# An exponential moved to an earlier table switch, gather rows for empty slots, and expert numbers loaded in two pieces

## The chip, the cores and the metric

The program runs on one core of one Trainium2 chip. The metric is the device time of one execution in microseconds (us). The decoder has six stages; the change touches only the third, the first expert layer.

## What is computed

The reference is a decoder of two layers on x of shape (8, 256, 128), which are 2,048 tokens of width 128. The stage at hand is the routed and shared feed-forward of the first layer:

```
D_MODEL, HIDDEN, E_ROUTED, E_SHARED, TOP_K = 128, 256, 14, 2, 2
def _ffn(xn, rw, W1, W2):
    h = xn * rsqrt(mean(xn * xn) + RMS_EPS) * rw
    return silu(h @ W1) @ W2
```

Each token goes through both shared experts and through the two of 14 routed experts with the largest router logits. The routed results are weighted by gates: a softmax over the 14 logits, of which the two chosen are kept and divided by their sum. A layer norm of x plus this sum ends the stage.

## The kernel before

**The routing.** Tokens are sorted by expert into slots, 128 to a tile. NT is 45, the most tiles that 4,096 choices can need when each of 14 experts ends with a tile that is not full. VectorE (DVE) finds the rank of each choice (`RANK`, `TOTAL`, lines 1579 to 1629), and TensorE (PE) sums one-hot matrices into `SLOT_TOK`, the token number of each slot (line 2311). A slot that nobody has stays at 0, and so it names token 0. `tok` (line 1631) is the copy of these numbers, and `tei` (line 1635) holds for each tile the offset of its expert's weights.

**The gates.** DVE writes the scaled logits `Lg` (lines 1537 and 1541, semaphore `lg_sub`). ScalarE (ACT) takes the exponential (line 1063, semaphore `lg_exp`). The rest of the gates (`gates_step` 2 and on) is done by DVE between tiles 6 and 20 of the tile loop.

**The shared experts.** PE's `shared_up(n)` (line 2285), ACT's `shared_silu(n)` (line 1053) and PE's `shared_out(n)` (line 2291) run for n from 0 to 7 ahead of the tile loop, beside DVE's routing, and for n from 8 to 15 behind it. After each of the first eight Silus ACT normalizes two tiles of X (line 1069). The exponential stands behind Silu number 7, the last ahead of the tile loop. ACT's functions come in tables: an ACT_TABLE_LOAD stands in the trace where another table is loaded.

**The tile loop.** POOL issues one indirect DMA for each tile j (line 815), which gathers 128 rows of `xrows` into `XG[j % 4]` by `tok[:, j]`. For i from 0 to 47, PE issues in this order:

```
slot_up(i - 1)        # hidden = xTs @ W1E[expert], line 2346; waits for ACT's Silu of the tile before
experts_from(i)       # if i % 4 == 0: load the next 4 offsets from tei, line 2337
gather_T(i)           # transpose of XG, line 2333; waits for the gather
hidden_T(i - 2)       # lines 2352, 2353
slot_down(i - 3)      # y = hidden @ W2E[expert], line 2360
```

DVE copies the transposes out of PSUM (`xTs` line 1685, `hTs` line 1690), ACT takes the Silu into `hS` (line 1075) and copies `Y` (line 1081), and SP stores each Y. Ahead of its first tile ACT also copies the sums of the shared experts (`OT`, line 1057). When all Ys are stored POOL gathers them back (line 821).

The order on each engine is written out by hand. The functions that the diff touches:

Of the kernel before, what the change touches and what calls it, by code (L numbers as in the profile page):

```python
# [19 lines left out]
ACT = mybir.ActivationFunctionType  # L20
AX = mybir.AxisListType
F32 = mybir.dt.float32
# [3 lines left out]
F16 = mybir.dt.float16  # L26
# [4 lines left out]
T = N // 128  # L31
# [8 lines left out]
E1, I1, K1 = 64, 64, 8  # L40
NT = (2 * N + E0R * 127) // 128
RING = 4
SPLITS = 12
FAR = 8192.0
ROUND = 12582912.0
# [4 lines left out]
def decoder_program(nc, a, out):  # L50
# [28 lines left out]
        "route_consts": ("norm_done", B * PAIRS + 2),  # L79
        "route_init": ("split_done", B // 2 * SPLITS + 2),  # L80
        "yt_ready": ("fold_hi", 4),
        "xs_out": ("raw_in0", B * SPLITS // 4 * 16),
        "we_in": ("raw_in1", B * SPLITS // 4 * 16),
        "decay_out": ("split_out0", B * SPLITS // 4 * 16),
        "coef_out": ("split_out1", B * SPLITS // 4 * 16),
        "te_done": ("acc_free", B + 2),
# [4 lines left out]
        "sum_done": ("rms", 2 * NC_ + 2),  # L91
        "hot_j": ("w_rounded", B // 2 * SPLITS),
        "shared_added": ("bo_added", 4),
        "ya_in0": ("xg_in0", (NT + 3) // RING * 16),
        "ya_in1": ("xg_in1", (NT + 2) // RING * 16),
        "ya_in2": ("xg_in2", (NT + 1) // RING * 16),
        "ya_in3": ("xg_in3", NT // RING * 16),
        "diag_done": ("q_done", 4),
# [11 lines left out]
    def sem(name):  # L110
        name = COUNTS_ON[name][0] if name in COUNTS_ON else name
        if name not in sems:
            sems[name] = ctx.enter_context(nc.semaphore(name))
        return sems[name]

    def on(name, n):
        return COUNTS_ON[name][1] + n

    def sb(name, shape, dt=F32, scope=ctx):
        return scope.enter_context(nc.sbuf_tensor(name, shape, dt))  # L120

    with ctx:
        PS = ctx.enter_context(nc.psum_tensor("PS", [128, 8 * CH], F32))

        def bank(n, w=CH, k=1):
            return PS[:, n * CH:n * CH + (k - 1) * CH + w]
# [117 lines left out]
        sx = ExitStack()  # L244
        eqJ = sb("eqJ", [128, 2, NT, T], F16, sx)
        idJ = sb("idJ", [128, 2, NT, T], F16, sx)
# [1 line left out]
        iotaR = sb("iotaR", [128, 128, T], F16, sx)  # L248
        jslot16 = sb("jslot16", [128, 2, T], F16, sx)
        rslot16 = sb("rslot16", [128, 2, T], F16, sx)  # L250
        tokid16 = sb("tokid16", [128, T], F16, sx)
        cmpJ = sb("cmpJ", [128, NT, E0R], F32, sx)
        Lg = sb("Lg", [128, T, E0R], F32, sx)
        eqE = sb("eqE", [128, T, E0R], F32, sx)
# [11 lines left out]
        over = sb("over", [128, E0R, T], F32, sx)  # L266
# [8 lines left out]
        tok = sb("tok", [128, NT], U32, sx)  # L275
        iota128 = sb("iota128", [128, 128], F32, sx)
        iotaJ = sb("iotaJ", [128, NT], F32, sx)
        iotaK = sb("iotaK", [128, T], F32, sx)
        tokid = sb("tokid", [128, T], F32, sx)
        notfirst = sb("notfirst", [128, E0R, T], F32, sx)  # L280
        below = sb("below", [128, 128], F32, sx)
        XG = [sb(f"XG{r}", [128, 128], F32, sx) for r in range(RING)]
        xTs = [sb(f"xTs{r}", [128, 128], F32, sx) for r in range(2)]
        hS = [sb(f"hS{r}", [128, HID], F32, sx) for r in range(2)]
        hTs = [sb(f"hTs{r}", [128, HID], F32, sx) for r in range(2)]
        Y = [sb(f"Y{r}", [128, 128], F32, sx) for r in range(RING)]
        kTe = sb("kTe", [128, B * SC], F32, sx)
# [85 lines left out]
        SLOT_TOK = bank(7)[:, 256:256 + NT]  # L373
# [47 lines left out]
            return bank(4 + t // 4)[:, t % 4 * 128:t % 4 * 128 + 128]  # L421


        GATES_EXP = 7
        FIRST, LAST = 0, B // 2 - 1
        RANKS_AT, HOT_AT = 0, {5: (0, 1), 6: (2, 3)}
        STEPS = 2 * PAIRS
# [5 lines left out]
        def turn(n, c):  # L433
            return NC_ * n + c + (B - NC_ if n > 2 else 0)
# [232 lines left out]
        def _(pool):  # L667
# [8 lines left out]
                               base=0, pattern=[[-1, 128]], channel_multiplier=1).then_inc(sem("consts"), 1)  # L676
            pool.affine_select(out=cmask[:, 128:256], in_=cmask[:, 128:256], compare_op=ALU.is_ge, fill=BIG,
                               base=0, pattern=[[-1, 128]], channel_multiplier=1).then_inc(sem("consts"), 1)
            pool.affine_select(out=blockones[:, :], in_=blockones[:, :], compare_op=ALU.is_ge, fill=0.0,
                               base=0, pattern=[[-DX, HX], [0, DX]], channel_multiplier=1).then_inc(sem("zeroed"), 1)  # L680
            pool.wait_ge(sem("zeroed"), 4)
            pool.affine_select(out=blockones[:, :], in_=blockones[:, :], compare_op=ALU.is_ge, fill=0.0,
                               base=DX - 1, pattern=[[DX, HX], [0, DX]], channel_multiplier=-1).then_inc(sem("consts"), 1)
# [95 lines left out]
            for s in range(2):  # L779
# [2 lines left out]
            pool.iota(iota128[:, :], [[1, 128]], base=0, channel_multiplier=0, allow_small_or_imprecise_dtypes=True).then_inc(sem("route_consts"), 1)  # L782
            pool.iota(iotaJ[:, :], [[1, NT]], base=0, channel_multiplier=0, allow_small_or_imprecise_dtypes=True).then_inc(sem("route_consts"), 1)
            pool.iota(iotaK[:, :], [[128, T]], base=0, channel_multiplier=0, allow_small_or_imprecise_dtypes=True).then_inc(sem("route_consts"), 1)
            pool.iota(tokid[:, :], [[128, T]], base=0, channel_multiplier=1, allow_small_or_imprecise_dtypes=True).then_inc(sem("route_consts"), 1)
            pool.memset(notfirst[:, :, :], 1.0).then_inc(sem("route_init"), 1)
            pool.memset(below[:, :], -1.0).then_inc(sem("route_init"), 1)
            pool.memset(G20[:, :, :], NEG).then_inc(sem("route_consts"), 1)
# [4 lines left out]
                               base=0, pattern=[[-1, 128]], channel_multiplier=1).then_inc(sem("route_consts"), 1)  # L793
            pool.wait_ge(sem("route_consts"), on("route_consts", 8))
            pool.tensor_copy(iotaR[:, :, :], iota128[:, :].rearrange("p (r o) -> p r o", o=1).to_broadcast([128, 128, T])).then_inc(sem("route_consts"), 1)
            pool.tensor_copy(tokid16[:, :], tokid[:, :]).then_inc(sem("route_consts"), 1)

            for c in range(NC_):
                cc = slice(4 * c, 4 * c + 4)
# [10 lines left out]
            pool.wait_ge(sem("tok_done"), on("tok_done", 1))  # L810
            pool.wait_ge(sem("xs_out"), on("xs_out", 16 * NC_))
            for j in range(NT):
                if j >= RING:
                    pool.wait_ge(sem("xt_ready"), on("xt_ready", j - RING + 1))
                pool.indirect_dma_start(out=XG[j % RING][:, :], out_offset=None, in_=xrows,  # L815
                                        in_offset=bass.IndirectOffsetOnAxis(ap=tok[:, j:j + 1], axis=0)).then_inc(sem(f"xg_in{j % RING}"), 16)
# [95 lines left out]
        def _(act):  # L912
# [146 lines left out]
            for n in range(8):  # L1059
                shared_silu(n)  # L1060
                if n == GATES_EXP:
                    act.wait_ge(sem("lg_sub"), 1)
                    act.activation(Lg[:, :, :], Lg[:, :, :], ACT.Exp).then_inc(sem("lg_exp"), 1)
                if n % 2 == 0:
                    act.wait_ge(sem("ln_factor"), 2 * turn(1, n // 2) + 2)
                if n == 4:
                    act.wait_ge(sem("xs_late"), 8)
                for t in (2 * n, 2 * n + 1):
                    act.activation(X[:, t, :], X[:, t, :], ACT.Identity, scale=rs[:, t:t + 1], bias=nb[:, t:t + 1]).then_inc(sem("ln_x"), 1)

            def slot_silu(j):
                act.wait_ge(sem("hs_ready"), on("hs_ready", j + 1))
# [234 lines left out]
        def _(dve):  # L1307
# [195 lines left out]
            def after_last():  # L1503
                dve.wait_ge(sem("g_step"), steps[0])

            def done(instruction):
                instruction.then_inc(sem("g_step"), 1)
                steps[0] += 1
# [67 lines left out]
            flat2 = lambda x: x.rearrange("p e t -> p (e t)")  # L1576
# [35 lines left out]
            across = lambda x, w: x.rearrange("p (o t) -> p o t", o=1).to_broadcast([128, w, x.shape[-1]])  # L1612
# [6 lines left out]
            for s in range(2):  # L1619
                if s:  # L1620
                    same_tile(1)
                dve.wait_ge(sem("hot_j"), on("hot_j", s + 1))
                done(dve.tensor_tensor(idJ[:, s, :, :], eqJ[:, s, :, :], across(tokid16[:, :], NT), ALU.mult))
                after_last()
                for h in range(2):
                    tt = slice(8 * h, 8 * h + 8)
                    dve.tensor_tensor(eqH[:, s, :, tt], iotaR[:, :, tt], across(rslot16[:, s, tt], 128), ALU.is_equal).then_inc(sem("hot_done"), 1)
            done(dve.tensor_tensor(cmpJ[:, :, :], iotaJ[:, :].rearrange("p (j o) -> p j o", o=1).to_broadcast([128, NT, E0R]),
                                   ctile[:, :].rearrange("p (o e) -> p o e", o=1).to_broadcast([128, NT, E0R]), ALU.is_ge))
            dve.wait_ge(sem("tok_ready"), 1)  # L1630
            dve.tensor_copy(tok[:, :], SLOT_TOK).then_inc(sem("tok_done"), 1)  # L1631
            after_last()
            done(dve.tensor_reduce(te[:, :], cmpJ[:, :, :], AX.X, ALU.add))
            after_last()
            dve.tensor_scalar(tei[:, :], te[:, :], float(E0R - 1), float(HID), ALU.min, ALU.mult).then_inc(sem("te_done"), 1)
# [405 lines left out]
            with dve.Fori(2, E1 // 4) as i:  # L2041
                for k in range(8):
# [6 lines left out]
                    s, c = k // 4, k % 4  # L2049
# [11 lines left out]
        def _(pe):  # L2061
# [271 lines left out]
                pe.transpose(slot_xT, XG[j % RING][:, :], ident[:, :]).then_inc(sem("xt_ready"), 1)  # L2333

            def experts_from(j):
                n = min(NT - j, 4)
                _, e = nc.values_load_multi_w_load_instructions(
                    tei[0:1, j:j + n], engines=[mybir.EngineType.PE], min_val=0, max_val=(E0R - 1) * HID,
                    skip_runtime_bounds_check_because="a count of at least 0, bounded by ALU.min where tei is written")
                return {j + m: e[m] for m in range(n)}  # L2340
# [24 lines left out]
            for i in range(NT + 3):  # L2365
                if 1 <= i < NT + 1:
                    slot_up(i - 1, experts[i - 1])
                if i < NT:
                    if i % 4 == 0:
                        experts.update(experts_from(i))  # L2370
                    gather_T(i)
                if 2 <= i < NT + 2:
                    hidden_T(i - 2)
                if i >= 3:
                    slot_down(i - 3, experts.pop(i - 3))
                if 2 <= i < 4:
                    shared_T(i - 2, i - 2)
# [405 lines left out]
```

## Time and profile before

| | |
|---|---|
| runs | 954.63, 954.72, 957.13 us; median 954.72 |
| profiled execution | 955.09 us, span 953.0 us |
| busy | PE 883.2 us, DVE 779.8, ACT 557.4, POOL 419.4 |
| mean granted PE clock | 0.977 |
| tile loop, first to last transpose of XG | 332.3 to 404.1 us |

The span is the time from the first instruction to the last, and the 2.09 us beside it are start and end of the execution. Busy time of PE is not PE at its peak, since matmuls overlap. The chain of work says which engine each moment of the end time hung on.

### The profile page before, as it was taken

How to read it: one execution, taken by the hardware profiler on the slowest of the kernel's cores; microseconds unless marked ns; L12 is line 12 of the kernel's file. 1: busy time of each engine (PE TensorE's matmuls, PEld its weight loads, DVE VectorE, ACT ScalarE, POOL GpSimd, SP SyncE). 2: the span in 40 equal slices, each digit the busy share in tenths (PEclk: the TensorE clock that was granted, in tenths of full speed). 3: DMA queues.
4: the chain of work that ended last, by engine and by line, in shares of the span. 5: the costliest groups of instructions: out<-in, count | busy, mean ns of one | idle time of the engine just before them, and what ended most of it. 6: DMA issues, size and time to landing. Idle time of an engine off the chain costs nothing.

```text
span 953.0 us, 17273 instructions
## 1 busy us (share of the span) xinstructions
PE 883.2 (93%) x5277; PEld 720.8 (76%) x5277; DVE 779.8 (82%) x2047; ACT 557.4 (58%) x1323; POOL 419.4 (44%) x491
## 2 busy tenths in 40 slices
PE   6999999999998888889877999989999999999995
PEld 5888888888886467747765797876668888888883
DVE  5887888889988657728898999968599999999996
ACT  5666666667767543447874324356755565556555
POOL 6776767667766165456416577432710000000002
PEclk9999999999999899999998899999999999999998
DMA  8333323233225033511012211010056666666641
GB/s 310 114 112 98 108 94 122 96 102 114 92 96 182 6 73 84 76 47 34 23 46 90 73 61 45 1 50 17 6 155 182 182 174 177 174 179 173 181 137 44
DMA packets 47280, 98.46 MB, mean 103 GB/s; under 512 B 7137, under 2 KB 23585, under 8 KB 46194
## 3 DMA queue, kind: packets, MB, share of 16 engines
q1 hardware_dynamic: 44754, 92.64, 31.6%
q0 software_dynamic: 2464, 5.05, 2.9%
q8 instruction: 32, 0.52, 0.2%
q14 instruction: 30, 0.25, 0.1%
HBM read 75.25 MB, written 22.41 MB: 102 GB/s over the span
## 4 chain that ended last, share of the span: by engine, by line
PE 72%; DVE 15%; issue 6%; ACT 3%; DMA 2%; POOL 1%; another core or an unknown queue 1%; DVEq 0%; SPq 0%; POOLq 0%; ACTq 0%
PE PS L2063 16%; PE PS L2064 15%; PE PS L2065 15%; PE PS L2134 5%; PE PS L2122 5%; DVE rb L1860 3%; PE PS L2146 3%; PE PS L2360 3%; DVE keep L1841 2%; PE PS L2346 2%; PE PS L2285 2%; PE PS L2291 1%; DVE PS L1829 1%; DVE dfb L1846 1%; DMA W<-w3s 1%
## 5 line engine op out<-in xcount | busy, mean ns | idle before, releaser
L460 POOL TENSOR_TENSOR rs<-ms,neghalf 128x4 f32<-128x4 f32 (+1 forms) x28 | 26.0, 928 | 273.2 <-DVE nm L454 271.5
L708 POOL TENSOR_TENSOR P<-P,rl 128x256 f32<-128x256 f32 (+1 forms) x128 | 104.2, 835 | 71.0 <-DVE rl L1365 71.0
L1292 ACT ACTIVATE FG<-PS 128x512 f32<-128x512 f32 x112 | 66.9, 597 | 92.9 <-PE PS L2065 92.9
L941 ACT ACTIVATE P<-P,mn 128x128 f32<-128x128 f32 (+1 forms) x256 | 112.6, 444 | 0.4 <-DVE mn L1358 0.4
L2063 PE MATMUL PS<-XTh,W 128*128 128x512 f32 x256 | 100.5, 393 | 1.5 <-DMA W<-w3s 0.6
L2064 PE MATMUL PS<-XTl,W 128*128 128x512 f32 x256 | 99.7, 390 | 0.0
L2065 PE MATMUL PS<-XTh,W 128*128 128x512 f32 x256 | 99.7, 390 | 0.0
L2046 DVE TENSOR_TENSOR FU<-FG,PS 128x512 f32<-128x512 f32 x112 | 77.0, 688 | 17.4 <-ACT FG L1292 4.6
L1358 DVE CUSTOM_DVE_ANT_0 P<-PS,cmask 128x128 f32<-128x128 f32 (+1 forms) x256 | 75.9, 352 | 18.6 <-issue 18.4
L2029 DVE TENSOR_TENSOR FHL<-FH,FHH 128x512 fp32r<-128x512 f32 x128 | 89.9, 702 | 0.9 <-ACT FHH L1278 0.9
L948 ACT ACTIVATE Uh<-PS 128x512 fp32r<-128x512 f32 x64 | 38.3, 598 | 81.9 <-PE PS L2065 81.8
L1278 ACT ACTIVATE FHH<-FH 128x512 fp32r<-128x512 f32 x128 | 80.9, 632 | 8.2 <-DVE FH L2038 7.8
L1370 DVE COPY PT<-PS 128x768 f32<-128x768 f32 x64 | 60.3, 942 | 7.5 <-PE PS L2122 7.4
L815 POOL DMA_INDIRECT XG<-xrows,tok x45 | 42.8, 951 | 45.7 <-DVE tok L1631 19.0
L2063 PEld LDWEIGHTS PS<-XTh,W 128*128 128x128 f32 x256 | 48.0, 188 | 16.2 <-issue 5.9
L2065 PEld LDWEIGHTS PS<-XTh,W 128*128 128x128 f32 x256 | 48.1, 188 | 10.1
L2122 PE MATMUL PS<-ident,P 128*128 128x128 f32 x384 | 54.4, 278 | 1.0 <-POOL P L708 0.9
L850 POOL TENSOR_TENSOR gb<-gb,dfb 128x1020 f32<-128x1020 f32 x16 | 37.9, 2386 | 38.9 <-ACT dfb L1207 38.5
L2064 PEld LDWEIGHTS PS<-XTl,W 128*128 128x128 f32 x256 | 48.1, 188 | 9.1
L2063 PE MATMUL PS<-FHH,W 128*128 128x512 f32 x128 | 50.9, 398 | 1.1 <-DVE FHL L2029 0.8
L1388 DVE TENSOR_TENSOR Ul<-PS,Uh 128x512 fp32r<-128x512 f32 x64 | 44.2, 691 | 8.6 <-ACT Uh L948 0.2
L2065 PE MATMUL PS<-FHH,W 128*128 128x512 f32 x128 | 49.9, 390 | 0.0
(472 smaller groups left out, 2559.1 us busy)
## 6 DMA issues: line engine op xcount, KB each, us to landing
GI<-coef SPq DMA_DIRECT2D x56, 256.0 KB, 4.1
GW<-coef SPq DMA_DIRECT2D x56, 256.0 KB, 4.1
w3s<-WS SPq DMA_DIRECT2D x32, 384.0 KB, 2.6
W<-w3s SPq DMA_DIRECT2D x32, 384.0 KB, 3.3
Wb<-decay SPq DMA_DIRECT2D x7, 1024.0 KB, 4.7
WR<-in_w SPq DMA_DIRECT2D x32, 192.0 KB, 2.5
WR<-in_w SPq DMA_DIRECT2D x16, 256.0 KB, 2.9
w12f<-WS SPq DMA_DIRECT2D x16, 256.0 KB, 2.0
```

Of the source, the lines that this page charges most:

```text
L708: last = pool.tensor_tensor(v, v, f, ALU.mult)
L941: last = act.activation(P[:, slot, c:c + w], P[:, slot, c:c + w], ACT.Exp, scale=-1.0, bias=mn[:, par, q:q + 1], accum_out=ls[:, par, q:q ...
L1278: act.activation(FHH[:, (k - 1) % 4, :], FH[:, (k - 1) % 4, :], ACT.Copy).then_inc(sem("fhh_done"), 1)
L1292: act.activation(FG[:, k % 2, :], bank(4 + k % 2), ACT.Silu).then_inc(sem("fg_done"), 1)
L1358: dve.tensor_tensor_reduce(out=P[:, slot, c:c + w], in0=scores(par, q), in1=cmask[:, 256 - w:256], scale=1.0, scalar=3e38, op0=ALU.add, op ...
L1370: dve.tensor_copy(PT[:, k % 2, :, :], PTP).then_inc(sem("pt_done"), 1)
L2029: dve.tensor_tensor(FHL[:, (k - 1) % 4, :], FH[:, (k - 1) % 4, :], FHH[:, (k - 1) % 4, :].bitcast(F32), ALU.subtract).then_inc(sem("fhl_do ...
L2046: dve.tensor_tensor(FU[:, k % 2, :], FG[:, k % 2, :], bank(6 + k % 2), ALU.mult).then_inc(sem("ft_done"), 1)
L2063: pe.matmul(dst, l[0], r[0], start=start, stop=False, skip_group_check=skip)
L2064: pe.matmul(dst, l[0], r[1], start=False, stop=False, skip_group_check=skip)
L2065: return pe.matmul(dst, l[1], r[0], start=False, stop=stop, skip_group_check=skip)
L2122: last = pe.transpose(bank(4 + h)[:, j * 128:j * 128 + 128], P[:, slot, c:c + 128], ident[:, :])
```

## The change

Three edits, all in the first expert layer.

- The exponential of the gates moves from behind Silu number 7 to behind Silu number 0, after the two tiles of X that are normalized there. The tables are loaded by two explicit instructions, for Exp ahead of these normalizations and for Silu behind the exponential.
- The token numbers are written plus one, so that an empty slot shows as 0. The first 4 tiles get max(number - 1, 0), as before. In tiles 4 to 44 a slot with 0 gets its own partition's number p, so that its gather reads row p of `xrows` and not row 0. This makes three DVE instructions of one, and POOL waits for the second part ahead of tile 4. Empty slots' results are read by nobody.
- The offsets are loaded 23 and then 22 at a time (i = 0 and 23), where they were loaded 4 at a time (12 loads).

```diff
+READY_TILES = 4
+NE = (NT + 1) // 2
...
-        GATES_EXP = 7
+        GATES_EXP = 0
...
-            pool.iota(tokid[:, :], [[128, T]], base=0, channel_multiplier=1, ...)
+            pool.iota(nextid[:, :], [[128, T]], base=1, channel_multiplier=1, ...)
...
             for j in range(NT):
+                if j == READY_TILES:
+                    pool.wait_ge(sem("tok_done"), on("tok_done", 2))
                 if j >= RING:
                     pool.wait_ge(sem("xt_ready"), on("xt_ready", j - RING + 1))
...
             for n in range(8):
                 shared_silu(n)
                 if n == GATES_EXP:
-                    act.wait_ge(sem("lg_sub"), 1)
-                    act.activation(Lg[:, :, :], Lg[:, :, :], ACT.Exp).then_inc(sem("lg_exp"), 1)
+                    act.preload_act_table(ACT.Exp)
...
                 for t in (2 * n, 2 * n + 1):
                     act.activation(X[:, t, :], X[:, t, :], ACT.Identity, ...)
+                if n == GATES_EXP:
+                    act.wait_ge(sem("lg_sub"), 1)
+                    act.activation(Lg[:, :, :], Lg[:, :, :], ACT.Exp).then_inc(sem("lg_exp"), 1)
+                    act.preload_act_table(ACT.Silu)
...
-                done(dve.tensor_tensor(idJ[:, s, :, :], eqJ[:, s, :, :], across(tokid16[:, :], NT), ALU.mult))
+                done(dve.tensor_tensor(idJ[:, s, :, :], eqJ[:, s, :, :], across(next16[:, :], NT), ALU.mult))
...
-            dve.tensor_copy(tok[:, :], SLOT_TOK).then_inc(sem("tok_done"), 1)
+            dve.tensor_scalar(tok[:, 0:READY_TILES], SLOT_TOK[:, 0:READY_TILES], -1.0, 0.0, ALU.add, ALU.max).then_inc(sem("tok_done"), 1)
+            own_row = flat2(over[:, :, :])[:, READY_TILES:NT]
+            done(dve.scalar_tensor_tensor(own_row, SLOT_TOK[:, READY_TILES:], 0.0, nextid[:, 0:1].to_broadcast([128, NT - READY_TILES]), ALU.is_equal, ALU.mult))
             after_last()
+            dve.scalar_tensor_tensor(tok[:, READY_TILES:], SLOT_TOK[:, READY_TILES:], -1.0, own_row, ALU.add, ALU.add).then_inc(sem("tok_done"), 1)
             done(dve.tensor_reduce(te[:, :], cmpJ[:, :, :], AX.X, ALU.add))
...
-                n = min(NT - j, 4)
+                n = min(NT - j, NE)
...
-                    if i % 4 == 0:
+                    if i % NE == 0:
                         experts.update(experts_from(i))
```

## Rows read from the trace of the kernel before

**Rows 1.** The page: the span, and the chain that ended last by engine.

```profile
span 953.0 us, 17273 instructions
...
PE 72%; DVE 15%; issue 6%; ACT 3%; DMA 2%; POOL 1%; another core or an unknown queue 1%; DVEq 0%; SPq 0%; POOLq 0%; ACTq 0%
```

**Rows 2.** The chain of work around the start of the tile loop: start, length, what.

```profile
330.36 1.28 ACT L1063
...
331.65 0.39 ACT Lg L1063
332.04 0.77 ACT Xp L1069 x2
332.81 0.96 ACT OT L1057 x2
...
333.79 1.28 ACT L1075
...
335.08 0.39 ACT hS L1075
```

**Rows 3.** PE in order of time: start, length, what, and idle time with its releaser.

```profile
333.05 0.69 PE L2346 MATMUL PS<-W1E,xTs 128*128 x2 [0.46 <-DVE xTs L1685]
...
335.70 0.69 PE L2346 MATMUL PS<-W1E,xTs 128*128 x2 [1.85 <-ACT hS L1075]
```

**Rows 4.** ACT in order of time around the first two shared Silus.

```profile
310.98 0.60 ACT L1053 ACTIVATE Hf<-PS 128x512 f32<-128x512 f32 x1 [2.40 <-PE PS L2285]
...
316.77 0.60 ACT L1053 ACTIVATE Hf<-PS 128x512 f32<-128x512 f32 x1 [4.43 <-PE PS L2285]
```

**Rows 5.** DVE in order of time: scaled logits, then token numbers and expert offsets.

```profile
313.42 0.39 DVE L1541 TENSOR_TENSOR Lg<-Lg,rs 128x224 f32<-128x224 f32 x1
...
328.85 0.21 DVE L1631 CAST tok<-PS 128x45 uint32<-128x45 f32 x1 [2.97 <-PE PS L2311]
328.97 0.80 DVE L1633 TENSOR_REDUCE te<-cmpJ 128x45 f32<-128x630 f32 x1
329.81 0.19 DVE L1635 TENSOR_SCALAR tei<-te 128x45 int32<-128x45 f32 x1
```

**Rows 6.** The gathered tile XG: PE's transposes of it (ns min/median/max, first and last start).

```profile
L2333 PE MATMUL PS<-ident,XG x45: 272/273/329, 332.3 to 404.1; 128*128 128x128 f32 x45
```

**Rows 7.** PE in order of time in the tile loop, tiles 11 to 13, 34, 35 and 43.

```profile
351.11 0.27 PE L2333 MATMUL PS<-ident,XG 128*128 128x128 f32 x1
...
352.46 0.29 PE L2333 MATMUL PS<-ident,XG 128*128 128x128 f32 x1
...
353.97 0.68 PE L2360 MATMUL PS<-W2E,hTs 128*128 x4 [0.99 <-ACT Y L1081]
...
354.93 0.27 PE L2333 MATMUL PS<-ident,XG 128*128 128x128 f32 x1
...
387.44 0.27 PE L2333 MATMUL PS<-ident,XG 128*128 128x128 f32 x1
...
389.87 0.27 PE L2333 MATMUL PS<-ident,XG 128*128 128x128 f32 x1
...
402.78 0.33 PE L2333 MATMUL PS<-ident,XG 128*128 128x128 f32 x1 [0.57 <-DMA XG<-xrows,tok]
```

**Rows 8.** Loads of expert offsets (ns min/median/max, first and last start): all, the one-value load.

```profile
L2337 PEldq TENSOR_LOAD <-tei x12: 313/334/517, 330.4 to 403.6; - x12
...
L2337 PEldq TENSOR_LOAD <-tei x1: 313/313/313, 403.6 to 403.6; - x1
```

**Rows 9.** Stretches: length, busy (instructions) of PE, PEld, DVE, ACT, POOL, clock, DMA share, GB/s.

```profile
383.00:393.00 10.00, 8.82 (x59) 7.33 (x58) 6.64 (x24) 3.99 (x13) 5.85 (x7) 1.00 0.34 78
...
398.00:403.00 5.00, 3.99 (x26) 2.88 (x25) 3.45 (x9) 1.98 (x6) 0.88 (x1) 1.00 0.88 58
```

**Rows 10.** The chain of work at the loop's tail and behind it.

```profile
396.65 6.08 DMA XG<-xrows,tok
...
408.89 2.67 PE PS L2285 x6
```

More of the change, by code:

```diff
@@ L250, in decoder_program @@
         rslot16 = sb("rslot16", [128, 2, T], F16, sx)
-        tokid16 = sb("tokid16", [128, T], F16, sx)
+        next16 = sb("next16", [128, T], F16, sx)
         cmpJ = sb("cmpJ", [128, NT, E0R], F32, sx)
@@ L278, in decoder_program @@
         iotaK = sb("iotaK", [128, T], F32, sx)
-        tokid = sb("tokid", [128, T], F32, sx)
+        nextid = sb("nextid", [128, T], F32, sx)
         notfirst = sb("notfirst", [128, E0R, T], F32, sx)
@@ L784, in _ @@
             pool.iota(iotaK[:, :], [[128, T]], base=0, channel_multiplier=0, allow_small_or_imprecise_dtypes=True).then_inc(sem("route_consts"), 1)
-            pool.iota(tokid[:, :], [[128, T]], base=0, channel_multiplier=1, allow_small_or_imprecise_dtypes=True).then_inc(sem("route_consts"), 1)
+            pool.iota(nextid[:, :], [[128, T]], base=1, channel_multiplier=1, allow_small_or_imprecise_dtypes=True).then_inc(sem("route_consts"), 1)
             pool.memset(notfirst[:, :, :], 1.0).then_inc(sem("route_init"), 1)
@@ L795, in _ @@
             pool.tensor_copy(iotaR[:, :, :], iota128[:, :].rearrange("p (r o) -> p r o", o=1).to_broadcast([128, 128, T])).then_inc(sem("route_consts"), 1)
-            pool.tensor_copy(tokid16[:, :], tokid[:, :]).then_inc(sem("route_consts"), 1)
+            pool.tensor_copy(next16[:, :], nextid[:, :]).then_inc(sem("route_consts"), 1)
             for c in range(NC_):
```

## Prediction

> **What bounds the kernel now.** I read the page first. The chain that ended last is PE for 72% and DVE for 15% [rows 1], but that is an average over six stages, and the change touches only one, between about 311 and 409 us. So I read the chain of work and PE in order of time there. Three stretches of that stage matter.
>
> At the start of the tile loop the chain lies on ACT. Behind the last shared Silu it loads a table (1.28 us), takes the exponential (0.39), normalizes two tiles (0.77), copies two sums (0.96), loads the Silu table again (1.28), and only then takes the first tile's Silu at 335.08 [rows 2]. PE's second slot_up stands idle for 1.85 us until that Silu is there [rows 3].
>
> In the middle of the loop PE sets the pace. The transposes of XG, one a tile, follow each other at 1.35 us when nothing disturbs (351.11 to 352.46), which is PE's own work for a tile [rows 7]. All 45 take 404.1 - 332.3 = 71.8 us [rows 6], while 44 steps of 1.35 are 59.4 us. The other 12.4 us are disturbances. The largest kind looks like tile 12 to 13: 2.47 us, or 1.1 over the pace, in which slot_down idles 0.99 us for a copy of Y that itself waited for an earlier result of PE [rows 7]. I went through the 44 steps. Six are of that kind, from tiles 4, 12, 16, 20, 28 and 34, with 1.0 to 1.7 us over the pace each. Some others are 0.3 us over.
>
> At the loop's tail the chain hangs for 6.08 us on one gather, issued at 396.65 [rows 10]. In that stretch the DMA engines are 88% busy and move 58 GB/s. Ten us earlier, with the same size of gathers, they were 34% busy and moved 78 GB/s [rows 9]. The last tiles are the empty ones, and all their 128 slots name row 0, so repeated reads of one row are what I take as the cause.
>
> Behind the loop PE goes straight into the second half of the shared experts [rows 10]. So what the loop saves is passed on to the rest of the program, which has no part in the change.
>
> **Part 1, the exponential.** Removed from the stretch before the loop: one table load (1.28) and the exponential (0.39) behind Silu 7, and the Silu load (1.28) ahead of the first tile, 2.95 us of ACT work [rows 2]. The gain is smaller than that, since other waits come next. The copies of the two sums need the last shared_out, which ends at about 332.3, just ahead of the first transpose of XG [rows 6]. They then take 0.96 and end at 333.3. The first tile's Silu needs slot_up, which starts at 333.05 and takes 0.69, so it can start at about 333.8 [rows 3]. It starts at 335.08 now. The gain is 335.08 - 333.8 = 1.3 us. What is late next is PE, then the gathers: POOL issues the first eight 1.25 us apart, slightly faster than PE's 1.35, so I count nothing for them.
>
> What is added lies beside the first two Silus. Silu 0 ends at 311.58 and Silu 1 starts at 316.77, with ACT idle for 4.43 us because it waits for PE [rows 4]. The added sequence is: table load 311.6 to 312.9, two normalizations to 313.7 (0.77), the wait for the logits that DVE ends at 313.81 [rows 5], exponential to 314.3, table load to 315.5. That leaves 1.2 us of cover. Should it be gone, each us past it delays Silu 1, and shared_out 1 behind it. Nobody needs the exponential before tile 6.
>
> **Part 2, rows for empty slots.** The first part of `tok` is a short tensor_scalar in place of the 0.21 us copy [rows 5]. The nearest small DVE instruction is the tei one, 0.19 us, so the first gather starts as before. Two more DVE instructions of about 0.2 us and a wait of 0.05 lie ahead of te and tei: +0.45 us, and tei ends at 330.45 and not at 330.0. PE's first load of offsets starts at 330.4 now and is the longest of the twelve, 0.52 [rows 8]; and the next thing on PE is the first transpose at 332.3, which waits for its gather [rows 6]. The load would end at about 331.4, so 0.9 us of cover is left and the cost is nothing. POOL's new wait ahead of tile 4 is over by about 329.5, while the fifth gather is issued at 334.6. Nothing queues behind it.
>
> The gain is at the tail. The steps 39 to 43 are 1.80, 1.42, 1.93, 2.05 and 1.32 us, together 1.8 over the pace; for two of them PE waits in so many words for the gather, 0.44 us at tile 42 and 0.57 at tile 43 [rows 7]. Lower bound 0, if the slowness has another cause. Upper bound 1.8. I take 1.2, since the first 0.45 came while its gather had long landed.
>
> **Part 3, two loads for twelve.** The instruction itself is cheap: 334 ns in the median, nearly all for four values [rows 8], and at tile 12 the transposes around it are on the pace, 351.11 and 352.46 [rows 7]. So by the direct cost, ten loads are worth about nothing. But the disturbance of 1.1 us follows at once. Of the six long ones five (tiles 4, 12, 16, 20, 28) come in the tile that has a load, though only one tile in four has one; and five loads (tiles 8, 24, 32, 36, 40) have none behind them. The sixth, tile 34 to 35 (387.44 to 389.87), looks the same and has no load near [rows 7]. I read this as a hold-up of PE's results that arises by itself every two to four tiles, short (0.3 us) when nothing else is there and long when a load falls into it. Lower bound of the gain: 0, if the holds don't care about the loads. Upper bound: the five long ones whole, 1.74 + 1.11 + 1.00 + 0.96 + 1.11 = 5.9 us. If each turned into a short one, 5.9 - 1.5 = 4.4. The case of tile 34 says that long ones come without loads too, so I take 2.5.
>
> The new loads carry 23 and 22 values. The median of 334 ns is that of loads of four values, and the one of a single value took 313 [rows 8]: 7 ns for each further value, which makes about 0.5 us for 23. The first is under the cover of part 2, the second costs at most 0.5 at tile 23, inside the 2.5.
>
> The Trainium skill (Runtime: NRT & Kernel Launch, section Instruction fetch mechanics) gives about 200 ns per register for a load of registers, even in bulk. The trace does not agree: four values would be 0.8 us, and the row has 0.33. What the skill's figure would make of the sum is given with the rivals.
>
> **The sum.** 1.3 + 1.2 + 2.5 = 5.0 us. The profiled execution has 955.09 us (span 953.0 and 2.09 around it), which becomes 950.1. It is 0.37 above the median of the runs, so against the median of 954.72 the forecast is 949.7. Less than about 0.3% (2.9 us) can't be told from no change in this kernel.
>
> **The rivals.**
> - *The holds don't care about the loads.* Then part 3 gives 0 to 0.9 and the sum is 1.0 to 3.4 us: about 952.3, between 951.3 and 953.7. For it: tile 34, and the five loads without a hold. It also covers that a loop without loads runs into its holds more often: 16 to 20 was four tiles at 1.6 us each, and the whole loop at that rate would give back some 1.5 us. Against it: five of six. Chance 0.37.
> - *The holds need the loads altogether.* All the excess between tiles 4 and 39 goes, some 7 us, and the sum is 8 to 10: about 945.5. Against it: tile 34 and the short ones. Chance 0.09.
> - *Repeated reads are not the cause of the slow tail.* Parts 1 and 3 are left, 3.8 us: 950.9. For it: only that no row shows a gather of 128 distinct rows with this neighbourhood. Against it: the same gathers ran at 34% share just before [rows 9]. Chance 0.05. The edit would then not do what it says.
> - *The long loads stop PE* (the other side). If the values are fetched one after another at the price of the one-value load, 0.313 us [rows 8], the first takes 7.2 us and ends at 337.7, 5.4 after 332.3, and the second adds 6.9 at tile 23. With the 5.0 of gain that is 7.3 slower: 962.0. It decides from about 0.2 us for each value. Against it: four values cost as much as one. Chance 0.05.
>
> By the 200 ns of the Trainium skill (Runtime: NRT & Kernel Launch, Instruction fetch mechanics) the loads would take 4.6 and 4.4 us, which ends at about 957; the trace's 334 ns for four values speaks against it.
>
> **How the numbers follow.** The forecast (sum 3.5 to 8, 946.7 to 951.2) has 0.44. The likeliest single time is 949.7. The range must leave out no more than 2 in 10: from 945.5 (most of the second rival) to 953.4 (most of the first). Faster by over 0.3% needs a gain of 2.9: the forecast 0.44, the second rival 0.09, of the first about 0.05, of the third 0.03, together 0.61. Slower by over 0.3% is the last rival and whatever the phase of PE's clock in the later stages may cost: 0.05. Within 0.3%: 0.34.
>
> **What the profile after would show.** Part 1: two table loads between Silu 0 and Silu 1 near 312 and 315, none between 329 and 400, and hS of tile 0 at about 333.8. Part 2: the last steps at the pace, no wait for XG there, a DMA share of about 0.35 up to the end of the loop, tei at about 330.5. Part 3: two TENSOR_LOADs of about 0.5 us; fewer or shorter holds, and the first to the last transpose in 67 to 68 us and not 71.8. The prediction is wrong if the holds stand as many and as long in a loop without loads, or if a TENSOR_LOAD of 23 values is long.

## The result, and the profile after

The changed kernel takes 961.45 us in the median of four runs (959.77 to 962.88), the kernel before 954.71 beside it (954.63 to 957.13, four runs). The ratio is 1.0068, 95% interval 1.0047 to 1.0090: it is slower, by 6.5 us at that ratio. The forecast was 949.7 with a range of 945.5 to 953.4, so the sign is wrong, and of the rivals the one to which I gave 0.05 has come closest (962.0).

The profiled execution took 959.77 us. First the page, to be held against [rows 1]:

```profile
span 957.8 us, 17266 instructions
...
PE 71%; DVE 13%; issue 6%; ACT 4%; POOL 3%; DMA 2%; another core or an unknown queue 1%; SPq 0%; DVEq 0%; POOLq 0%; ACTq 0%
```

It says nothing of the cause: the shares are nearly those of before. The two other edits did what was said. ACT in order of time around the first two Silus, for [rows 4]:

```profile
312.21 0.60 ACT L1057 ACTIVATE Hf<-PS 128x512 f32<-128x512 f32 x1 [2.52 <-PE PS L2295]
312.83 1.28 ACT L1066 ACT_TABLE_LOAD   x1
314.12 0.88 ACT L1072 ACTIVATE Xp<-Xp,nb,rs 128x128 f32<-128x128 f32 x2
314.94 0.39 ACT L1075 ACTIVATE Lg<-Lg 128x224 f32<-128x224 f32 x1
315.35 1.28 ACT L1076 ACT_TABLE_LOAD   x1
317.87 0.60 ACT L1057 ACTIVATE Hf<-PS 128x512 f32<-128x512 f32 x1 [1.24 <-PE PS L2295]
```

All of the exponential's work lies in the gap between Silu 0 and Silu 1, and 1.24 us of cover is left (1.2 was forecast). PE's first slot_ups, for [rows 3]:

```profile
334.82 0.69 PE L2356 MATMUL PS<-W1E,xTs 128*128 x2 [0.46 <-DVE xTs L1695]
...
336.17 0.69 PE L2356 MATMUL PS<-W1E,xTs 128*128 x2 [0.55 <-DVE xTs L1695]
```

They are 1.35 us apart and were 2.65: 1.3 us gained, as in the sum. Then two stretches near the loop's end, for [rows 9] (length, busy of PE, PEld, DVE, ACT, POOL, clock, DMA share, GB/s):

```profile
389.00:399.00 10.00, 9.38 (x63) 7.90 (x61) 7.05 (x25) 4.48 (x14) 5.91 (x7) 1.00 0.31 83
404.00:409.00 5.00, 4.93 (x33) 4.20 (x33) 4.09 (x13) 2.31 (x8) 1.58 (x2) 1.00 0.33 92
```

The last tiles' gathers now cost the DMA engines no more than the others do: share 0.33 and 92 GB/s, where it was 0.88 and 58. The chain has no wait for a gather there any more, where it had one of 6.08 us [rows 10].

The third edit is where the time went. The loads of offsets and the transposes (ns min/median/max, first and last start), for [rows 8] and [rows 6]:

```profile
L2347 PEldq TENSOR_LOAD <-tei x1: 2282/2282/2282, 331.6 to 331.6; - x1
...
L2347 PEldq TENSOR_LOAD <-tei x1: 5258/5258/5258, 371.8 to 371.8; - x1
...
L2343 PE MATMUL PS<-ident,XG x45: 272/273/447, 334.1 to 410.1; 128*128 128x128 f32 x45
```

The load of 23 values takes 2.28 us and that of 22 takes 5.26, where I had 0.5 for each. The 45 transposes take 76.0 us; 67 to 68 were forecast, and 71.8 it was before. PE in order of time at the second load, for [rows 7], and the stretch behind it:

```profile
371.01 0.27 PE L2343 MATMUL PS<-ident,XG 128*128 128x128 f32 x1
...
371.83 0.69 PE L2356 MATMUL PS<-W1E,xTs 128*128 x2
377.27 0.45 PE L2343 MATMUL PS<-ident,XG 128*128 128x128 f32 x1 [4.75 <-issue]
...
379.65 0.42 PE L2343 MATMUL PS<-ident,XG 128*128 128x128 f32 x1
...
381.13 0.27 PE L2343 MATMUL PS<-ident,XG 128*128 128x128 f32 x1
```

```profile
376.80:380.20 3.40, 2.93 (x12) 2.67 (x13) 1.25 (x5) 0.59 (x2) 0.94 (x1) 0.50 0.10 26
```

PE idles for 4.75 us with "issue" as the reason, which is to say that its own queue was busy, with the load. Then it works for 3.4 us at a granted clock of 0.50, the lower of its two levels (1.2 GHz), after having stood idle. The step from tile 22 to 23 takes 377.27 - 371.01 = 6.26 us and the next 2.38, which is 4.91 and 1.03 over the pace of 1.35. The first load delays the first transpose by 0.8 (it stands 3.7 us behind the first gather's issue, and 2.9 before). Together 6.7 us lost, 1.3 gained at the first tiles, and 1.6 at the tail, whose steps 39 to 43 take 6.94 us and took 8.52: 3.8 us.

There is a second stretch at half clock, with no load near. At tiles 4 and 5 two PE instructions wait 0.84 and 1.00 us, and then PE works at 0.50 up to about 346.1 (transposes, and the stretch):

```profile
339.70 0.27 PE L2343 MATMUL PS<-ident,XG 128*128 128x128 f32 x1
...
343.82 0.42 PE L2343 MATMUL PS<-ident,XG 128*128 128x128 f32 x1
...
346.13 0.27 PE L2343 MATMUL PS<-ident,XG 128*128 128x128 f32 x1
```

```profile
342.80:346.10 3.30, 3.30 (x13) 2.79 (x13) 1.57 (x4) 0.94 (x3) 1.16 (x2) 0.50 0.26 65
```

The steps from tiles 4 and 5 take 4.12 and 2.31 us, and 3.09 and 1.35 before: 2.0 us more. That these are a consequence of the change is not shown. In all, the time from the first gather's issue to the last transpose has grown by 5.0 us (79.7 from 74.7); ahead of it the profiled execution is 1.0 us longer, and behind it 1.2 us shorter.

The holds that I had put down to the loads are still there. The changed kernel has long steps from tiles 4, 12, 16 and 20, as the kernel before has, with loads at tiles 0 and 23 only.

### The profile page after: what moved, and what is told of

Same layout as the page of the kernel before. It is cut to its first block, busy times and chain, and to the rows that moved or that the text cites. A ratio compares the mean times of both kernels' runs of the same rounds, so it can differ in the third digit from the quotient of the medians.

```text
span 957.8 us, 17266 instructions
## 1 busy us (share of the span) xinstructions
PE 887.8 (93%) x5277; PEld 727.4 (76%) x5277; DVE 780.8 (82%) x2049; ACT 556.7 (58%) x1323; POOL 419.4 (44%) x491
## 4 chain that ended last, share of the span: by engine, by line
PE 71%; DVE 13%; issue 6%; ACT 4%; POOL 3%; DMA 2%; another core or an unknown queue 1%; SPq 0%; DVEq 0%; POOLq 0%; ACTq 0%
PE PS L2073 15%; PE PS L2075 14%; PE PS L2074 14%; PE PS L2144 5%; PE PS L2132 5%; PE PS L2370 3%; PE PS L2156 3%; DVE rb L1870 2%; PE PS L2356 2%; DVE keep L1851 2%; PE PS L2295 1%; PE PS L2301 1%; DMA WR<-in_w 1%; DMA W<-w3s 1%; DVE dfb L1856 1%
```

## Experiments

Ratios are against the kernel before on the same chip, with 95% intervals. Kernels without a ratio ran once, so their times have no interval. The runs fell on several chips, and that turned out to matter: the kernel before takes 954.4 to 954.7 us on some of them (three at least) and 943.8 (one run) and 944.9 on two others. Each chip had one batch of runs, so chip and batch are not told apart. A "hold" is a step of the loop that is about 1 us over the pace because PE's results come late.

**The parts by themselves.** Each is that part of the change's diff and nothing else. For the kernel with the first two parts:

```diff
 READY_TILES = 4
-NE = (NT + 1) // 2
+NE = 4
```

*The exponential alone.* 

> The kernel before with part 1 alone. If part 1 is worth what was forecast, the first tile's Silu starts 1.3 us earlier against the first transpose of XG and the time falls by 1.3 us, to about 953.4. Rival, that the tighter start costs something (a hold-up in the first tiles, or a half-speed stretch of PE's clock there): no gain or a loss, 954.7 or more.

Measured: 954.65, ratio 1.0001 (0.9987 to 1.0015). The first slot_ups are 1.35 us apart, but the third and the fifth step have become longer, 1.90 and 3.55 where they were 1.35 and 3.09. Of the 1.3 us about 0.2 is left by then. From the first gather's issue to the last transpose the loop takes 73.65 us and took 74.73, and what stands behind it takes 550.5 in this execution and took 548.9.

*The rows for empty slots alone.* 

> The kernel before with part 2 alone. If repeated reads of row 0 slow the tail, steps 39 to 43 of the loop fall from 8.5 us together to about 6.8 and the time by 1.2 to 1.8, to about 953.2. Rival, that the two more DVE instructions delay the first tile: the first transpose of XG is 0.4 us later and nothing is gained.

Measured: 953.5, ratio 0.9985 (0.9973 to 0.9997), 1.4 us faster; the tail's steps are 1.35 to 1.40.

*The two long loads alone.* 

> The kernel before with part 3 alone. If the long loads are what made the changed kernel slower, it takes all of the loss and what parts 1 and 2 gave back: 6.7 + 2.8 = 9.5 us, about 964, with loads of 2 to 5 us again. Rival, that parts 1 or 2 have a share in the loss: below 960.

Measured: 958.18, ratio 1.0038 (1.0023 to 1.0052). Loads of 2.28 and 5.26 us, the step of tile 22 is 6.26. So this edit alone makes the kernel slower, by 3.6 us. That is far from the 9.5 that I expected, and about half of what the changed kernel loses: beside the other two parts the loads cost more than alone.

*The first two parts, loads of four.* 

> The changed kernel with four values a load again, so parts 1 and 2 without 3. If the long loads are the loss: 1.3 + 1.5 = 2.8 us below the kernel before, about 951.9. Rival, that another part is the loss: 956 or more.

Measured: 954.46, ratio 1.0004 (0.9991 to 1.0018). Without the long loads the loss is gone, but the 2.5 us forecast for the other two parts aren't there: the interval allows 0.9. In its trace the first gather to the last transpose takes 73.73 us, 1.0 less than before.

**Do the holds hang on the loads, or on PE's instructions?** Loads of 8 and of 12 values, no loads at all, and more waits per tile, each in the kernel before:

```diff
-                n = min(NT - j, 4)
+                n = min(NT - j, 8)      # or 12, 16
...
-                    if i % 4 == 0:
+                    if i % 8 == 0:      # or 12, 16
```

```diff
-                    if i % 4 == 0:
-                        experts.update(experts_from(i))
+                    experts[i] = 0      # and constant offsets in slot_up and slot_down
```

```diff
+                for _ in range(10):
+                    pe.wait_ge(sem("te_done"), on("te_done", 1))
```

> The kernel before with 8 values a load (6 loads). Loads of 4 took 0.33 us, of 22 and 23 values 5.26 and 2.28. If a load's price goes by its number of values, loads of 8 take 0.6 to 1.8 us each. If it stays flat up to some number, they take 0.35 us. The time stays within 3 us of before either way.

> The kernel before with 12 values a load (4 loads). By the number of values: 1.1 to 2.8 us each in the loop, at 0.1 to 0.24 us for each value. If the second long load was slow because of what runs beside it in the loop, the loads at tiles 12, 24 and 36 take twice as long as the one at tile 0 or more. If it was slow for another reason, all of 12 values take the same.

> The kernel before with every tile using the first expert's weights at a fixed place: no loads of offsets and no address arithmetic on PE, and the routed results are other than the reference's. If the holds of PE's results come from the loads, they go and the loop runs at 1.35 us a tile from tile 5 on, some 8 us less. If they don't, the mean stays near 1.58 us a tile. If they come from the rate at which PE takes instructions (about 25 records a tile), 2 to 3 fewer a tile give about 1.4 to 1.45.

> The kernel before with ten more waits a tile on PE, for a semaphore that has long been reached (five more sequencer instructions a tile, 0.05 us each, beside the wait for xTs). If the mean step is set by the number of PE's instructions (25 a tile in 1.58 us), 30 a tile make it 1.9 us and the loop 14 us longer. If not, it stays between 1.6 and 1.7.

Measured, with before at 954.45: 956.46, 959.34, 952.49 and 961.02. A load of 8 takes 0.60 us in most cases, one of 12 takes 0.86 and 0.96 behind the first tile. The third kernel has no load and shorter steps, 1.24 us when nothing disturbs, but its loop is no faster than 1.56 a tile, because it has as many holds and longer ones (2.5 to 2.6 us steps). Its transposes take as long as those of before:

```profile
L2333 PE MATMUL PS<-ident,XG x45: 272/273/421, 330.9 to 401.6; 128*128 128x128 f32 x45
```

So the holds do not need loads, which ends my reading of "five of six". The fourth kernel has an undisturbed step of 1.48 us and a mean of 1.66 from tile 5 to 21: its ten more waits do not stretch the mean to the 1.9 that a price for each of PE's instructions would give. Of the 6.6 us that it is slower, about 3.1 lie in the loop (77.9 us from the first gather's issue to the last transpose) and 3.7 behind it, where nothing was changed (552.5 us, and 548.9 before); why, no run shows.

**Loads of 16, gathers off POOL, six small loads at once.** These three fell on a chip where before takes 943.8 us.

> The kernel before with 16 values a load (16, 16 and 13, at tiles 0, 16 and 32). Loads of 4, 8 and 12 values in the loop took 0.33, 0.60 and 0.9 us, about 0.07 us for each value past the fourth. If that line goes on, 16 values take 1.15 us in the loop and 1.3 at tile 0. If a steeper part begins between 12 and 22 values, as 2.28 and 5.26 us for 23 and 22 say, they take 1.5 us or more; and if it is the second load that is slow, the one at tile 16 takes over twice the one at tile 0.

> The kernel before with the rows of XG brought by SP's queue, 128 rows in order and not by token, where POOL issued indirect gathers; the routed results are other than the reference's. All variants so far ran tiles 5 to 39 at 1.55 to 1.66 us each, with holds of PE's results between steps of 1.24 to 1.48. If the gathers issued by POOL cause the holds, they go and the mean is about 1.36. If PE's own work or the stores of Y do, the mean stays at 1.57.

> The changed kernel's grouping (23 values at tile 0, 22 at tile 23) on the kernel before, but each group fetched by six loads of up to four values in a row. If the price belongs to the single long instruction, six times 0.33 us, 2.0 us in all at either place. If it belongs to the number of values fetched at one place, the group at tile 23 takes 5 us again.

```diff
-            for j in range(NT):     # POOL: indirect_dma_start by tok[:, j]
+            def rows_in(j):         # SP: rows in their order
+                sp.dma_start(XG[j % RING][:, :], xrows[j % 16 * 128:j % 16 * 128 + 128, :]) ...
```

```diff
+                for k in range(j, min(NT, j + 23), 4):
+                    n = min(NT, j + 23, k + 4) - k      # a load of n <= 4, six at j = 0, six at j = 23
```

Measured: 945.63, 940.25 and 951.4. None of the three has a hold. From tile 4 on their loops run at the pace of 1.35, but for the steps at the loads and, where empty slots read row 0, the last ones. Gathers that POOL issues do not suffice for a hold, then. Whether they have a part in the holds on the other chips is not shown, since the kernel without them ran only here, where no kernel has holds. The loads of 16 take 1.30 us (the first) and 1.12, and the last, of 13, takes 1.12. The six small loads at tile 0 take 0.53, 0.35, 0.34, 0.33, 0.33 and then 0.77 for three values; those at tile 23 take 1.01, 1.15, 1.00, 1.00, 1.00 and 0.53. They do the same work as the six before and cost three times as much. So it isn't the length of one load that makes 22 values dear.

**What makes a load dear?** Four kernels with other groups of values. A correction to their expectations, which speak of the changed kernel: all four are the kernel before with its loads regrouped and nothing else (neither the exponential's move nor the rows). What they say of single loads isn't touched by it, but their times are to be held against the kernel before and against the long loads alone (958.18), and not against the changed kernel.

```diff
-                n = min(NT - j, 4)
+                n = STARTS[j]           # GROUPS = [23, 4, 4, 4, 4, 4, 2], or [4, 4, 4, 4, 4, 3, 22],
...                                      # or [24, 21], or [6, 4, 4, 4, 4, 4, 4, 4, 4, 4, 3]
-                    if i % 4 == 0:
+                    if i in STARTS:
```

> The changed kernel with the same first load of 23 expert numbers ahead of tile 0, but from tile 23 on in loads of 4 as in the kernel before (six small loads). Theory A, the number of values in one load sets its price: the 23 take 2.28 us as before and the small ones about 0.33 us each; the half-clock stretch behind tile 22 goes and the time falls by 5 to 7 us against the changed kernel. Theory B, once 23 values have been loaded every later load is dear (0.25 us per value): the small ones take about 1.0 us each, as the six small loads at tile 23 did, and the time stays within 3 us of the changed kernel's.

> The mirror image: loads of 4 for tiles 0 to 22 as in the kernel before, then one load of 22 ahead of tile 23. Theory A, 22 values in one load are dear by their number: 5.3 us at tile 23 as in the changed kernel. Theory B, only an earlier long load makes the second dear: about 22 x 0.07 = 1.5 us, and no half-clock stretch behind it. Theory C, the place (tile 23, in the midst of the loop's work) makes it dear: 5.3 us too, so A and C are not told apart by this run alone but by the small loads at the same place in the first kernel of this call.

The times are 946.42 and 951.71, with before at 944.92. The loads in the first kernel (23; the five of 4; the 2) and in the second (five of 4; the 3; the 22):

```profile
L2340 PEldq TENSOR_LOAD <-tei x1: 2289/2289/2289, 329.5 to 329.5; - x1
...
L2340 PEldq TENSOR_LOAD <-tei x5: 1002/1003/1122, 363.5 to 387.7; - x5
...
L2340 PEldq TENSOR_LOAD <-tei x1: 534/534/534, 393.7 to 393.7; - x1
```

```profile
L2340 PEldq TENSOR_LOAD <-tei x5: 330/336/529, 329.9 to 354.5; - x5
...
L2340 PEldq TENSOR_LOAD <-tei x1: 772/772/772, 360.0 to 360.0; - x1
...
L2340 PEldq TENSOR_LOAD <-tei x1: 5268/5268/5268, 364.4 to 364.4; - x1
```

Neither theory stands. Small loads are dear from tile 23 on (against A), and the 22 values are dear with no long load before them (against B). Nor is it the moment in the loop (C), since 16 values at tile 16 take 1.12 us. What fits nearly all of them is the place of the first value. From a multiple of four, each whole four costs about 0.28 us and each value left over 0.26; from another place, every value costs about 0.25. By it 23 from 0 is 5 x 0.28 + 3 x 0.26 = 2.18 (2.28 measured; a first load takes 0.1 to 0.2 more than later ones), 22 from 23 is 5.5 (5.26), 4 from 23 is 1.0 (1.00), 3 from 20 is 0.78 (0.77), 13 from 32 is 1.10 (1.12). Beside the 22, the worst fit is the last load of the kernel with loads of 8, 5 values from 40: 0.54 by the rule, and 0.72 measured. The other two kernels put it to the test.

> The changed kernel with its expert numbers in two loads of 24 and 21 in place of 23 and 22, so that the second begins at value 24, a multiple of four. The durations so far (4 values 0.33, 8 0.60, 12 0.86, 16 1.12, 13 beginning at 32 1.12; but 22 beginning at 23 5.26, 4 beginning at 23 1.0, 3 beginning at 20 0.77) fit a rule: from a first value whose place is a multiple of four, each whole four costs about 0.28 us and each left over 0.26; from another place every value costs about 0.25. By it the loads take 24: 6 x 0.28 = 1.7 us, and 0.2 more as a first load, and 21: 5 x 0.28 + 0.26 = 1.7 us, the half-clock stretch behind the second goes, and the kernel is about 4 us faster than the changed one. Rival, the number of values or the registers that they go to make the second dear: 5 us at tile 23 again, a half-clock stretch behind it, and the changed kernel's time.

> The changed kernel with a first load of 6 values and then loads of 4 that begin at 6, 10, 14 and so on, never at a multiple of four; no load is long. By the rule of the place (fours only from a multiple of four) the first takes 0.28 + 2 x 0.26 + 0.2 = 1.0 us and each of the others 1.0 us in place of 0.33; if pairs count too, each of the others takes about 0.55. Rival, an earlier long load makes later ones dear: 0.33 us each here.

```profile
L2340 PEldq TENSOR_LOAD <-tei x2: 1705/1756/1808, 331.3 to 372.5; - x2
```

```profile
L2340 PEldq TENSOR_LOAD <-tei x11: 763/1002/1123, 329.3 to 401.4; - x11
```

Both as by the rule: 24 values in 1.81 us and 21 in 1.71 with no stretch at half clock behind them; and 1.0 us for each four values from 6, 10, 14 and so on, though no load there is long. One value more in the first load makes the second three times cheaper. The kernel with 24 and 21 takes 957.06, ratio 1.0019 (1.0007 to 1.0032). That is half the loss of 23 and 22 (1.0038), and still 1.8 us slower than twelve loads of four. In the traces the loop has lost nearly all of its excess: from the first gather's issue to the last transpose it takes 75.4 us, against 78.9 with 23 and 22 and 74.7 before. Behind it this execution takes 550.9 us and that of before 548.9. The kernel that begins at 6 ran once, 956.41.

**The changed kernel and loads of four, on other chips.**

> The changed kernel once more, beside the kernel before and the variant with loads of 4 on the same chip. If this chip has the slow steps of the loop (about 1.57 us a tile): +6 to 7 us against before. If it is one without them (1.35 us a tile, before near 944 us): the loads of 2.3 and 5.3 us stand bare on the path, and it is slower than before by 4 to 7 us, unless the exponential's 1.3 and the rows' 1.2 us, absorbed elsewhere, come through: then by 2 to 5 us.

> The changed kernel with loads of 4 (its exponential and its rows alone), once more. On a chip with the slow steps: within 1 us of before, as measured at 1.0004. On one without them: theory A, the slow steps had absorbed the two gains: 1.3 + 1.2 = 2.5 us faster, ratio about 0.9974. Theory B, the gains are lost in later stages whatever the chip: within 0.5 us of before.

> The changed kernel with loads of 4 once more, for the comparison with loads of 24 and 21 on one chip. Twelve small loads cost 12 x 0.33 = 4.0 us, the two long ones 1.9 + 1.7 = 3.6 us by the rule of the place: the two kernels are within 1 us of each other. Against before: ratio 0.9965 if the chip is one without the slow steps, 1.000 if it has them.

On the chip where before takes 944.92, the changed kernel takes 947.6, ratio 1.0027 (1.0011 to 1.0043), and the one with loads of four 942.06, ratio 0.9965 (0.9947 to 0.9984). On a chip where before takes 954.6 the latter takes 955.99, ratio 1.0001 (0.9983 to 1.0020). The long loads cost much more beside the two other parts (947.6 - 942.06 = 5.5 us) than alone (3.6 us, on another chip). One reason is in the traces: alone, the first load takes 0.5 us off the wait that the exponential leaves at tile 1, where the step is 2.14 us and not 2.65. The rest of the difference is open. The transposes of the changed kernel and of the one with loads of four, both on the chip of 944.92:

```profile
L2343 PE MATMUL PS<-ident,XG x45: 272/273/445, 332.8 to 398.5; 128*128 128x128 f32 x45
```

```profile
L2343 PE MATMUL PS<-ident,XG x45: 272/273/328, 331.9 to 392.6; 128*128 128x128 f32 x45
```

65.7 and 60.7 us for 44 steps, and the second is 1.38 a step, nearly the pace. The first two parts pay here: 2.9 us between the medians (1.5 to 5.0 by the interval), where I had forecast 2.5. Against the kernel with groups 4, 4, 4, 4, 4, 3, 22 on the same chip, which has neither part, the two steps at tiles 1 and 2 take 3.15 and not 4.02 (0.9 us), and those at tiles 40 to 43 take 5.43 and not 7.56 (2.1 us).

**What a hold is.** Instructions from the transpose of tile 15 on, ahead of the long step from tile 16 to 17 (2.28 us), in the changed kernel on the first chip, and the same instructions in the changed kernel on the chip of 944.92:

```profile
359.96 0.27 PE L2363 MATMUL PS<-ident,hS 128*128 128x128 f32 x1
...
361.16 0.42 DVE L1700 COPY hTs<-PS 128x256 f32<-128x256 f32 x1 [0.81 <-PE PS L2363]
...
361.90 0.28 ACT L1088 ACTIVATE Y<-PS 128x128 f32<-128x128 f32 x1 [1.58 <-PE PS L2370]
```

```profile
353.50 0.27 PE L2363 MATMUL PS<-ident,hS 128*128 128x128 f32 x1
...
353.81 0.43 DVE L1700 COPY hTs<-PS 128x256 f32<-128x256 f32 x1
...
354.26 0.28 ACT L1088 ACTIVATE Y<-PS 128x128 f32<-128x128 f32 x1 [0.39 <-PE PS L2370]
```

In the second, DVE copies 0.31 us after PE's transpose has started. In the first it does so 1.20 us after, with nothing else to do, and ACT's copy of Y is late with it. PE's results arrive late for both engines at once. This comes every few tiles in each trace from the chips where before takes 954.4 us and more, and in none of the seven from the two others, the changed kernel among them.

## Why the prediction was wrong

- **The price of the long loads: the step that failed.** "7 ns for each further value, which makes about 0.5 us for 23" was drawn from two rows, four values (334 ns) and one (313 ns) [rows 8]. What I took for a small slope was, by the rule above, the price of a whole four against that of a single value. The loads take 2.28 and 5.26 us, and they alone make the kernel 3.6 us slower. The rival "the long loads stop PE" had the mechanism: PE's queue stands still and PE with it. It "decides from about 0.2 us for each value"; the second load had 0.24. Its own price of 0.313 for each value was too high, 7.2 and 6.9 us.
- **The cover.** "Transposes around it are on the pace" [rows 7] was read rightly, and its meaning missed. A load of 0.33 costs its tile almost nothing. On the chips without holds, loads of 1.00 us lengthen two steps together by 0.6 (2.01 + 1.30 against 2.70), of 1.12 by 0.7, and one of 5.27 its own step by 4.9. Some 0.35 to 0.4 us of each load is hidden. Twelve small loads use that cover twelve times, and two long ones twice. This fits that 24 and 21, 3.5 us of loads in place of some 4.2, win nothing in the loop (0.7 us more than before). It is not shown to be the cause of the whole 1.8 us.
- **The gain of part 3, 2.5 us.** Wrong altogether. The step was "I read this as a hold-up of PE's results that arises by itself [...] and long when a load falls into it". The kernel without loads has as many holds and as long ones, and the changed one has them at tiles 4, 12, 16 and 20 without a load there. The first rival (0.37) had this right; five of six was a coincidence, helped by a period near that of the loads.
- **The half clock behind the second load.** Not in the sum. The step behind the load, at a clock of 0.50, costs another 1.03 us. The other stretch at half clock, at tiles 4 to 6, was not in the sum either, and with the hold ahead of it costs 2.0 us more than tiles 4 and 5 took before. It is in none of the traces of the parts by themselves; what brought it stays open.
- **The first load's cover.** "About 0.9 us of cover" ahead of the first transpose was right as far as it went: 2.28 us of load delay it by 0.8.
- **Part 1, 1.3 us.** Right in its place, 2.65 to 1.35. Where holds occur nothing of it can be told at the end: 1.0001 (0.9987 to 1.0015). Where there are none, about 0.9 is left behind tile 2.
- **Part 2, 1.2 us.** The cause (one row read again and again) and the size hold: ratio 0.9985 alone, which is 1.4 us, and 2.1 us of shorter steps on a chip without holds. The middle that I chose, 1.2, lies inside the interval (0.3 to 2.6 us).
- **"What the loop saves is passed on."** Shown on the chips without holds only: 2.9 us there. On the others the first two parts together give nothing that can be told (1.0004 and 1.0001). In their traces the first gather to the last transpose takes 73.7 and 73.6 us, 1.0 to 1.1 less than before (74.7). So of 2.5 us less than half reaches the end of the loop, and it is not seen behind it, where the profiled executions on these chips take anything from 547.7 to 553.0 us, the kernel before 548.9. That the holds take the first part of it back fits the mean step from tile 5 to 21, 1.57 us in the kernel without loads and 1.59 before, though an undisturbed step takes 1.24 in the one and 1.35 in the other. But with an undisturbed step of 1.48 it is 1.66, so the holds are no fixed pace, and how a gain gets lost, in the loop and behind it, stays open.

The Trainium skill (Runtime: NRT & Kernel Launch, section Instruction fetch mechanics) gives about 200 ns per register for a load of registers, even in bulk. I set it aside on the strength of four values in 0.33 us. The runs are near it for loads that begin off a multiple of four (5258 / 22 = 239 ns) and far below it for the others (1116 / 16 = 70 ns). The sum of 957 us by that figure came nearer than mine.

## What to carry to other kernels

Two points near each other are no slope: where a change makes something five times as large, ask what the price would be if it were counted in other units than the ones the trace shows, and let that rival weigh. Many short instructions that each hide in a gap need not be improved by one long instruction that fills it once and then stands bare. And where a regular disturbance coincides with a regular instruction, count how often chance would do that before you put a price on it.

The version to keep is the change with its loads left at four: 942.06 against 944.92 us on a chip without holds, and no difference that can be told where they occur.

## What was not expected of the hardware

- A load of offsets into PE's registers costs about 0.28 us for each four values if the first one's place is a multiple of four, and about 0.25 us for each single value if it is not: 21 values from place 24 in 1.71 us, 22 from place 23 in 5.26. Whether the place in the tile decides, the address behind it, or the registers that the values go to was not separated: in every kernel the place of a value is also the number of values loaded before it.
- The same kernel takes 954.4 to 954.7 us on some chips and 943.8 and 944.9 on two, and in this loop the difference shows as late arrivals of PE's results, about 0.9 us each. With both first parts and loads of four the loop's 44 steps take 71 us on the one sort and 60.7 on the other. The cause stays open: the late arrivals need no loads, and more waits on PE did not raise the mean step as a price for each instruction would. Whether POOL's gathers have a part was not tried on a chip that has them.
- After 4.75 us of idleness PE ran at a clock of 0.50 for 3.4 us, on either sort of chip (0.51 on that of 944.92). After the 1.33 us that it idled for the load of 21 it did not. The idle time ahead of it doesn't settle it alone: in the kernel with loads of 16, PE waited 1.87 us for ACT near tile 1 and then ran at 0.50 (335.7 to 339.0), and in the kernel before it waited 1.85 us at the same place and stayed at 1.00 (336.0 to 339.0).
